# Queries of the third layer taken without waiting for scores, and the last attention item interleaved with the out blocks by halves

## The chip, the cores and the metric

One core of one Trainium2 chip runs one program. The metric is the device time of one execution in microseconds; the kernel before took 1414.33 us (median of 3 runs, 1413.99 to 1415.4). TensorE, ScalarE, VectorE and GpSimd are called PE, ACT, DVE and POOL below, as in the profile; SP is the queue that issues the weight loads.

## The reference, cut to what matters

Activations x have 4 images of 16 x 16 tokens with 1024 channels. Four layers follow each other, each `x = x + layer(group_norm(x))`.

```python
# layer 0: lambda layer     # layer 1: masked attention, 16 heads of 64, then Wo
# layer 2: attention, 16 heads of 64, with relative positions in rows and columns
qkv = x @ qkv_w + qkv_b
attn = (q * hd**-0.5) @ k.T            # per image and head, 256 x 256
rel_h = einsum('bhwc,hkc->bhwk', q, Rh); rel_w = einsum('bhwc,wkc->bhwk', q, Rw)
attn = softmax(attn + rel_h[..., None] + rel_w[..., None, :])
out = (attn @ v) @ proj_w + proj_b
# layer 3: 3 x 3 convolution of every channel, then four small cores that are
# one 1024 x 1024 channel matrix M, bias, relu
```

The change touches layer 2 (the third) and the seam between it and layer 3.

## The kernel before

Channels lie on partitions, tokens along the free dimension. Float32 products are made of three matmuls (high by high, low by high, high by low), so a weight block of 128 output channels by 1024 inputs costs 8 chunks of 3 matmuls over 512 tokens. Weights come in half blocks of 128 x 512 (4 chunks), through three slots of SBUF: SP loads the raw half block once POOL has split the one before it in that slot, POOL splits it into high and low (L212, L214) once PE has finished with the slot (`w_wait_used`), and PE waits for `w_ready`. The order of the half blocks is the list `sources`, written by `take`, and SP, POOL and PE all go through it in that order.

Attention of layers 1 and 2 is 32 items of two heads by two images: four stages of 8 items, stages 0 and 1 for layer 1 and stages 2 and 3 for layer 2. After a stage's 8 items come its 8 out blocks (`out_block(s, o, chunks)`), whose sums DVE adds to xT (`add_out`, L1403), with the statistics of the next group norm (`stats_of`) behind each.

Each engine's order is written out by hand. PE runs item i as: scores(i, 0), Q of item i+1 (`project`), transposes of the values (`turn_values`), the rest of Q, transposes of the probabilities (`turn_probs`, L1096), part of K, `attend(i, 0)` (L1112), scores(i, 1) (L1076), `relative(i + 1)` (64 small matmuls, L1140 and L1141), the rest of K, and V. `relative(i + 1)` waits for `q_hi`, which ACT raises when it has copied the queries of item i+1 from bank 0 to qp (`evac_q`, L1264). ACT runs item i as: evac_v, evac_o(i - 1), exps(i, 0), evac_t(i, 0) (the transposed probabilities), evac_q(i + 1), exps(i, 1) and so on; evac_q first waits for `s_done` of all scores of item i:

```python
            product_done(act, (i, "Q"))
            if i:
                act.wait_ge(s_done, 4 * i)
```

The last item (31) has no next item. There PE runs scores(31, 0), the rest of V, scores(31, 1), and then pieces of out blocks 0 and 1 of stage 3 between the transposes and products of the item. scores(31, 1) waits for `p_exp`, exps(31, 0) on ACT, which stand behind evac_v(31) and evac_o(30). Out blocks of stage 3 alternate between PSUM banks 0 and 1, so block o waits for the sum of block o - 2. Into blocks 2 to 7 the building of M is woven: `build_m(k)`, 16 pieces of two matmuls (L1168) into banks 4 and 5, two after the first half of a block and one after the second; ACT takes the high part (`head_of_m`, L1500), DVE the low part (`rest_of_m`, L1507), and piece k waits for the low part of piece k - 2. POOL makes the factors in BD (`masked_factor`, L1491), one for every four pieces.

Then PE runs `channel_product(0)` to `(3)` (L1534, 96 matmuls each) with `convolution` (L1551) between. Products of image 0 use banks 0 to 3 and wait for all sums of stage 3 on banks 0 and 1. DVE and ACT first do the group norm of images 2 and 3 (statistics, coefficients, then 8 times y, head, rest: L381, L379, L387, L392), and only then take image 0's products out of PSUM (L1586, L1612); channel_product(1) waits for that, bank by bank (`u_lo`).

Of the kernel before, what the change touches and what calls it, by code (L numbers as in the profile page):

```python
# [30 lines left out]
CK = C // P  # L31
HALF = 512
PAIRS = 8
# [32 lines left out]
def build(nc, A, out):  # L66
    outer = ExitStack()
    with outer:
# [98 lines left out]
        def take_item(i, halves=range(2)):  # L167
            for kind in "QKV":
                take((i, kind), STAGES[i // PAIRS][0], kind, i % PAIRS, halves)
# [3 lines left out]
        for i in range(ITEMS):  # L173
            if i + 1 < ITEMS:
                take_item(i + 1)
            if i % PAIRS == PAIRS - 1:
                for o in range(CK):
                    take((i // PAIRS, "O", o), STAGES[i // PAIRS][0], "O", o)

        slot_of, turn_of, landed_at, before_it = [], [], [], []  # L180
# [495 lines left out]
def later_layers(nc, A, out, outer, g):  # L676
# [301 lines left out]
    def layer_of(i):  # L978
        return STAGES[i // PAIRS][0]
# [26 lines left out]
        return PT if (i, kind) == (0, "V") else PJ[kind]  # L1006

    def out_bank(s, o):
        return (0 if s == 3 else O) + o % 2

    def product_done(eng, key):
        w_wait_used(eng, slots[key, 1])
# [1 line left out]
    def attention_pe(pe):  # L1014
# [128 lines left out]

        def out_block(s, o, chunks):
            for c in chunks:
                if c == 0 and o >= 2:
                    pe.wait_ge(sum_done, CK * s + o - 1)
                if c == 0 and o == 0 and s < 3 or o < 2 and c == CK - 1:
                    pe.wait_ge(o_hi, PAIRS * (s + 1))
                    pe.wait_ge(o_lo, PAIRS * (s + 1))  # L1150
                if c == 0 and o == 1 and s in (1, 2):
                    pe.wait_ge(relh_evac, PAIRS * (s - 1) + 1)
                    pe.wait_ge(relw_evac, PAIRS * (s - 1) + 1)
                if c == 0 and o == 0 and s == 3:
                    pe.wait_ge(v_evac, ITEMS)
                    pe.wait_ge(o_hi, ITEMS - 1)
                    pe.wait_ge(o_lo, ITEMS - 1)
                chunk_of((s, "O", o), c, lambda hl, c: (oh, ol)[hl][:, c, :], out_bank(s, o))

        def build_m(i):  # L1160
            if i >= 16:
                return
            if i % 4 == 0:
                pe.wait_ge(bd_ready, i // 4 + 1)
            if i >= 2:
                pe.wait_ge(m_lo, i - 1)
            for s in range(2):
                m = nc.tensor.matmul(PS[:, PT + i % 2, s * 256:s * 256 + 256], BD[:, (i // 4) % 2, (2 * i + s) % 8, :],  # L1168
                                     ttA[:, :], start=True, stop=True)
            m.then_inc(m_done, 1)  # L1170
# [31 lines left out]
        attend(i - 1, 1)  # L1202
        scores(i, 0)
        project(i, "V", range(4, CK))
        scores(i, 1)
        out_block(3, 0, range(0, 3))
        turn_values(i)
        turn_probs(i, 0)
        out_block(3, 0, range(3, 6))
        attend(i, 0)  # L1210
        out_block(3, 0, range(6, 7))
        out_block(3, 1, range(0, 2))
        turn_probs(i, 1)
        out_block(3, 1, range(2, 4))
        attend(i, 1)
        out_block(3, 1, range(4, 7))
        for o in range(2):
            out_block(3, o, range(7, CK))
        for o in range(2, CK):
            out_block(3, o, range(0, 4))  # L1220
            for k in range(2):
                build_m(3 * (o - 2) + k)
            out_block(3, o, range(4, CK))
            build_m(3 * (o - 2) + 2)

    def attention_act(act):
        def evac_v(i):
# [19 lines left out]
        def evac_t(i, a):  # L1247
            w = P * len(tiles(i))
            for n in (4 * i + 2 * a, 4 * i + 2 * a + 1):
                act.wait_ge(t_done, n + 1)  # L1250
                if n >= 4:
                    act.wait_ge(o_done, n // 2 - 1)
                nc.scalar.activation(probT[:, n % 4, 0:w], PS[:, PT + n % 2, 0:w], ACT.Copy).then_inc(t_evac, 1)  # L1253

        def evac_q(i):
            if i == ITEMS:
                return
            product_done(act, (i, "Q"))
            if i:
                act.wait_ge(s_done, 4 * i)  # L1260
            if layer_of(i) == 1:
                nc.scalar.activation(qh, PS[:, PJ["Q"], :], ACT.Copy).then_inc(q_hi, 1)
            else:
                nc.scalar.activation(qp, PS[:, PJ["Q"], :], ACT.Identity, bias=bias[:, i % PAIRS:i % PAIRS + 1]).then_inc(q_hi, 1)  # L1264
# [37 lines left out]
        for i in range(ITEMS):  # L1302
            evac_v(i)
            if i % PAIRS:
                evac_o(i - 1)
            exps(i, 0)
            evac_t(i, 0)
            evac_q(i + 1)
            exps(i, 1)
            evac_relative(i + 1)  # L1310
            evac_k(i + 1)
            evac_t(i, 1)
            if i % PAIRS == PAIRS - 1:
                evac_o(i)
            if 1 <= i % PAIRS <= 4:
                for c in (2 * (i % PAIRS) - 2, 2 * (i % PAIRS) - 1):
                    norm.y(nc.scalar, i // PAIRS + 1, c)
                for c in (2 * (i % PAIRS) - 2, 2 * (i % PAIRS) - 1):
                    norm.head(i // PAIRS + 1, c)
# [11 lines left out]
    def attention_dve(dve):  # L1331
# [81 lines left out]
        for i in range(ITEMS):  # L1413
            s, j = i // PAIRS, i % PAIRS
            maxima(i, 0)
            if j:
                rest_of_o(i - 1)
            normalize(i, 0)
            take_v(i)
            if j == 0:  # L1420
                norm.group_stats(s + 1)
            maxima(i, 1)
            rest_of_q(i + 1)
            normalize(i, 1)
            take_relative(i + 1)
            if i + 1 < ITEMS:
                rest_of_k(i + 1)
            if j == PAIRS - 1:
                rest_of_o(i)
            if j == 0:  # L1430
                norm.coefficients(s + 1)
            if 1 <= j <= 4:
                for c in (2 * j - 2, 2 * j - 1):
                    norm.y(nc.vector, s + 1, c)
                for c in (2 * j - 2, 2 * j - 1):
                    norm.rest(s + 1, c)
            if j == PAIRS - 1:
                for o in range(CK):
                    if s == 3 and o >= 2:
                        rest_of_m(dve, 3 * (o - 2))  # L1440
                        rest_of_m(dve, 3 * (o - 2) + 1)
                    add_out(s, o)
                    if o:
                        stats_of(s, o - 1)
                    if s == 3 and o >= 2:
                        rest_of_m(dve, 3 * (o - 2) + 2)
                stats_of(s, CK - 1)
                norm.aggregate(s + 2, range(CK), 16)

# [12 lines left out]
    def attention_pool(pool):  # L1462
        for n in range(SLOTS0 + 2, len(sources)):
            w_split(pool, n)
            if n == slots[(1, "Q"), 0]:
                pool.wait_ge(w_ready, n + 1)
                nc.gpsimd.memset(qa[64:96, :, :], 0.0).then_inc(zeroed, 1)
                pool.wait_ge(zeroed, 1)
            for s in range(4):
                if n == slots[(PAIRS * s + 1, "K"), 0]:  # L1470
                    norm.power(s + 1)
            if n == slots[(ITEMS - 4, "Q"), 0]:
                masked_factor(pool, 0)
                masked_factor(pool, 1)
            for k in (2, 3):
                if n == slots[(3, "O", 0), 0] + 4 * k:
                    masked_factor(pool, k)
        norm.power(5)


# [19 lines left out]
        nc.scalar.activation(hi, src, ACT.Copy).then_inc(m_hi, 1)  # L1500

    def rest_of_m(dve, i):
        if i >= 16:
            return
        dve.wait_ge(m_hi, i + 1)
        src, hi, lo = m_views(i)
        nc.vector.tensor_tensor(lo, src, hi.bitcast(F32), ALU.subtract).then_inc(m_lo, 1)  # L1507
# [11 lines left out]
    def last_pe(pe):  # L1519
        pe.wait_ge(m_lo, 16)  # L1520

        def channel_product(b):
            for tt in range(2):
                for half in range(2):
                    bank = 2 * tt + half
                    if b:
                        pe.wait_ge(u_lo, 4 * (b - 1) + bank + 1)
                    elif bank < 2:
                        pe.wait_ge(sum_done, 4 * CK)
                    for c in range(CK):  # L1530
                        if b == 2 and bank == 0:
                            norm.ready(5, c)
                        for k, (hl, w) in enumerate(((0, Mh), (0, Ml), (1, Mh))):
                            m = nc.tensor.matmul(PS[:, bank, :], x3(hl, b, c, tt * P), w[:, c, half * HALF:half * HALF + HALF],  # L1534
                                                 start=c == k == 0, stop=c == CK - 1 and k == 2)
                    m.then_inc(u_done, 1)
# [260 lines left out]
```

## Time and profile before

| | |
|---|---|
| median of 3 runs | 1414.33 us |
| profiled execution | 1415.18 us, of it span 1413.4 us |
| PE busy | 1346.5 us, 95% of the span |
| DVE, ACT, POOL busy | 44%, 31%, 44% |
| mean granted TensorE clock | 0.989 |
| 16 waits of L1140 on ACT L1264 | 13.4 us |
| from the end of V's matmuls of item 31 to the end of the last out block | 61.0 us |

Matmul ends in the trace are modelled: a matmul of 512 columns shows about 0.40 us, while the next starts 0.23 us after it. So distances below are taken from start to start; for a group of n matmuls with one duration, the last start is the group's end less one duration.

### The profile page before, as it was taken

How to read it: one execution, taken by the hardware profiler on the slowest of the kernel's cores; microseconds unless marked ns; L12 is line 12 of the kernel's file. 1: busy time of each engine (PE TensorE's matmuls, PEld its weight loads, DVE VectorE, ACT ScalarE, POOL GpSimd, SP SyncE). 2: the span in 40 equal slices, each digit the busy share in tenths (PEclk: the TensorE clock that was granted, in tenths of full speed). 3: DMA queues.
4: the chain of work that ended last, by engine and by line, in shares of the span. 5: the costliest groups of instructions: out<-in, count | busy, mean ns of one | idle time of the engine just before them, and what ended most of it. 6: DMA issues, size and time to landing. Idle time of an engine off the chain costs nothing.

```text
span 1413.4 us, 20625 instructions
## 1 busy us (share of the span) xinstructions
PE 1346.5 (95%) x7792; PEld 1055.7 (75%) x7792; DVE 617.2 (44%) x1385; ACT 439.1 (31%) x1053; POOL 626.4 (44%) x715
## 2 busy tenths in 40 slices
PE   4899889799999999999999999999999999999998
PEld 3688755468888888888888777777877777677787
DVE  6423422674655324565423354433244444347322
ACT  2220112033534302353320344434024444334222
POOL 2332179035555466455556444434654534445100
PEclk9999989999999999999999999999999999999999
DMA  5111135012222232222223211211321212111012
GB/s 191 38 46 45 30 64 88 0 46 77 75 61 76 69 95 83 68 71 65 75 74 91 61 53 60 60 54 55 91 72 62 59 53 61 53 53 31 1 52 68
DMA packets 57122, 89.23 MB, mean 63 GB/s; under 512 B 6880, under 2 KB 19840, under 8 KB 57024
## 3 DMA queue, kind: packets, MB, share of 16 engines
q1 hardware_dynamic: 55024, 84.59, 21.3%
q10 hardware_dynamic: 2000, 3.32, 0.7%
q8 instruction: 63, 1.03, 0.3%
q14 instruction: 35, 0.29, 0.1%
HBM read 79.50 MB, written 4.19 MB: 59 GB/s over the span
## 4 chain that ended last, share of the span: by engine, by line
PE 82%; DVE 2%; ACT 1%; issue 1%; POOL 0%; ACTq 0%; DVEq 0%; POOLq 0%
PE PS L1022 50%; PE PS L1534 5%; PE PS L1076 4%; PE PS L1096 3%; PE PS L858 3%; PE PS L1112 2%; PE PS L876 2%; PE PS L1064 2%; PE PS L864 2%; PE PS L1122 2%; PE PS L1141 2%; PE PS L1551 2%; DVE part L842 1%; PE PS L1087 1%; ACT part L1264 1%
## 5 line engine op out<-in xcount | busy, mean ns | idle before, releaser
L1022 PE MATMUL PS<-XB,w_hi 128*128 128x512 f32 x1024 | 354.0, 405 | 1.0 <-POOL w_lo L214 1.0
L212 POOL CAST w_hi<-w_raw 128x512 fp32r<-128x512 f32 x195 | 123.0, 631 | 407.7 <-PE PS L1022 296.9
L214 POOL TENSOR_TENSOR w_lo<-w_raw,w_hi 128x512 fp32r<-128x512 f32 x195 | 254.3, 1304 | 15.6
L1022 PEld LDWEIGHTS PS<-XB,w_hi 128*128 128x128 f32 x1024 | 192.5, 188 | 44.4 <-issue 2.1
L1022 PE MATMUL PS<-XB,w_lo 128*128 128x512 f32 x512 | 202.2, 395 | 0.0
L1022 PE MATMUL PS<-XB,part 128*128 128x512 f32 x768 | 199.3, 403 | 0.0
L1022 PEld LDWEIGHTS PS<-XB,part 128*128 128x128 f32 x768 | 140.8, 188 | 30.5
L1243 ACT ACTIVATE part<-PS,nmax 128x256 f32<-128x256 f32 (+1 forms) x256 | 111.0, 448 | 165.6 <-DVE nmax L1340 108.7
L212 POOL CAST part<-part 128x512 fp32r<-128x512 f32 x85 | 53.0, 623 | 155.8 <-PE PS L1022 155.8
L1340 DVE TENSOR_REDUCE nmax<-PS 128x2 f32<-128x512 f32 x64 | 43.9, 690 | 170.0 <-PE PS L1076 170.0
L1022 PE MATMUL PS<-part,w_hi 128*128 128x512 f32 x344 | 112.8, 396 | 1.6 <-POOL w_lo L214 1.6
L214 POOL TENSOR_TENSOR part<-part,part 128x512 fp32r<-128x512 f32 x85 | 111.0, 1306 | 6.8
L1253 ACT ACTIVATE part<-PS 128x384 f32<-128x384 f32 (+1 forms) x128 | 62.7, 543 | 163.6 <-PE PS L1096 163.6
L1022 PEld LDWEIGHTS PS<-XB,w_lo 128*128 128x128 f32 x512 | 96.5, 189 | 18.6 <-issue 0.2
L1337 DVE TENSOR_REDUCE nmax<-PS 128x1 f32<-128x128 f32 (+1 forms) x128 | 36.8, 350 | 153.1 <-PE PS L1069 153.1
L1350 DVE TENSOR_SCALAR part<-part,prec 128x256 f32<-128x256 f32 (+1 forms) x256 | 94.5, 411 | 4.5
L1022 PEld LDWEIGHTS PS<-part,w_hi 128*128 128x128 f32 x344 | 65.3, 190 | 16.2 <-DVE xT L1403 2.0
L635 PE MATMUL PS<-XB,w_hi 128*128 128x512 f32 x256 | 72.0, 398 | 0.0
L1022 PE MATMUL PS<-part,w_lo 128*128 128x512 f32 x172 | 67.5, 392 | 0.0
L1076 PE MATMUL PS<-part,part 112*128 112x256 f32 x256 | 63.8, 392 | 3.1 <-ACT part L1243 3.1
L392 DVE TENSOR_TENSOR XB<-part,XB 128x512 fp32r<-128x512 f32 x40 | 42.4, 1091 | 50.7 <-ACT XB L387 50.7
L1022 PE MATMUL PS<-part,part 128*128 128x512 f32 x252 | 61.0, 390 | 0.0
(142 smaller groups left out, 2010.8 us busy)
## 6 DMA issues: line engine op xcount, KB each, us to landing
w_raw<-in_w SPq DMA_DIRECT2D x187, 256.0 KB, 2.6
part<-in_w SPq DMA_DIRECT2D x85, 256.0 KB, 2.6
part<-part SPq DMA_DIRECT2D x32, 128.0 KB, 4.3
out_x<-xT SPq DMA_DIRECT2D x16, 256.0 KB, 2.1
xT<-in_x ACTq DMA_DIRECT2D x8, 256.0 KB, 7.9
xT<-in_x SPq DMA_DIRECT2D x8, 256.0 KB, 10.7
w_raw<-in_w SPq DMA_DIRECT2D x16, 128.0 KB, 4.0
part<-in_emb ACTq DMA_DIRECT2D x1, 961.0 KB, 12.4
```

Of the source, the lines that this page charges most:

```text
L212: pool.tensor_copy(hi, raw).then_inc(w_hi_done, 1)
L214: pool.tensor_tensor(lo, raw, hi.bitcast(F32), ALU.subtract).then_inc(w_ready, 1)
L635: m = nc.tensor.matmul(PS[:, 2 * (n % 2) + h, :], wt[:, (c % 4) * P:(c % 4) * P + P], x_part(hl, h, c), start=c == k == 0, stop=c == CK - ...
L858: m = nc.tensor.matmul(bank[:, 0:DY * SIDE], lhs, rhs, start=jp == 0, stop=jp == 1)
L1022: m = nc.tensor.matmul(PS[:, bank, :], wt[:, (c % 4) * P:(c % 4) * P + P], rhs(hl, c), start=c == k == 0, stop=c == CK - 1 and k == 2)
L1076: m = nc.tensor.matmul(PS[:, S + hh, qt * N:qt * N + N], qa[:, hh, qs], ka[:, hh, a * N:a * N + N], start=True, stop=True)
L1096: m = nc.tensor.transpose(PS[:, PT + n % 2, at:at + P], prob[:, n % 4, qt, kt_ * P:kt_ * P + P], ident[:, :])
L1243: last = nc.scalar.activation(prob[:, n % 4, qt, lo:hi], PS[:, S + n % 2, qt * N + lo:qt * N + hi], ACT.Exp, bias=nmax[:, n % 4, qt:qt + 1 ...
L1253: nc.scalar.activation(probT[:, n % 4, 0:w], PS[:, PT + n % 2, 0:w], ACT.Copy).then_inc(t_evac, 1)
L1340: last = nc.vector.tensor_reduce(nmax[:, n % 4, :], PS[:, S + n % 2, :].rearrange("p (a n) -> p a n", a=2), AX, ALU.max, negate=True)
L1350: last = nc.vector.tensor_scalar(prob[:, n % 4, qt, lo:hi], prob[:, n % 4, qt, lo:hi], prec[:, n % 4, qt:qt + 1], None, ALU.mult)
L1534: m = nc.tensor.matmul(PS[:, bank, :], x3(hl, b, c, tt * P), w[:, c, half * HALF:half * HALF + HALF], start=c == k == 0, stop=c == CK - 1 ...
```

## The change

In layer 2 ACT copies the queries without a wait for scores, and before evac_t(i, 0) instead of behind it. (The first item of layer 2, item 16, is taken during item 15.) For the last stage, the half blocks of out blocks 0 to 2 come as three first halves and then three second halves; the first three chunks of out block 0 stand ahead of scores(31, 1); out blocks use three banks, 1, 7 and 0, in turn (block o waits for the sum of block o - 3, block 1 for the copy of the values out of bank 7); the 16 pieces of M follow the table M_AFTER; two of POOL's factors move in its queue; and image 0's products wait for the sums bank by bank.

```diff
@@ -173,8 +173,12 @@
         for i in range(ITEMS):
             if i + 1 < ITEMS:
                 take_item(i + 1)
+            if i == ITEMS - 1:
+                for half in range(2):
+                    for o in range(3):
+                        take((3, "O", o), 2, "O", o, (half,))
             if i % PAIRS == PAIRS - 1:
-                for o in range(CK):
+                for o in range(3 if i == ITEMS - 1 else 0, CK):
                     take((i // PAIRS, "O", o), STAGES[i // PAIRS][0], "O", o)
 
         slot_of, turn_of, landed_at, before_it = [], [], [], []
@@ -1006,7 +1010,11 @@
         return PT if (i, kind) == (0, "V") else PJ[kind]
 
     def out_bank(s, o):
-        return (0 if s == 3 else O) + o % 2
+        return (1, X, 0)[o % 3] if s == 3 else O + o % 2
+
+
+    M_AFTER = {(0, 0): (), (1, 0): (), (2, 0): (), (0, 1): (0, 1), (1, 1): (2, 3), (2, 1): (4, 5), (3, 0): (6,), (3, 1): (7,),
+               (4, 0): (8,), (4, 1): (9,), (5, 0): (10, 11), (5, 1): (12,), (6, 0): (13,), (6, 1): (14,), (7, 0): (15,), (7, 1): ()}
 
     def product_done(eng, key):
         w_wait_used(eng, slots[key, 1])
@@ -1143,23 +1151,23 @@
 
         def out_block(s, o, chunks):
             for c in chunks:
-                if c == 0 and o >= 2:
-                    pe.wait_ge(sum_done, CK * s + o - 1)
-                if c == 0 and o == 0 and s < 3 or o < 2 and c == CK - 1:
+                beside = 3 if s == 3 else 2
+                if c == 0 and o >= beside:
+                    pe.wait_ge(sum_done, CK * s + o - beside + 1)
+                if c == 0 and o == 0 and s < 3:
                     pe.wait_ge(o_hi, PAIRS * (s + 1))
                     pe.wait_ge(o_lo, PAIRS * (s + 1))
+                if s == 3 and o == 0:
+                    pe.wait_ge(o_hi, PAIRS * s + c + 1)
+                    pe.wait_ge(o_lo, PAIRS * s + c + 1)
                 if c == 0 and o == 1 and s in (1, 2):
                     pe.wait_ge(relh_evac, PAIRS * (s - 1) + 1)
                     pe.wait_ge(relw_evac, PAIRS * (s - 1) + 1)
-                if c == 0 and o == 0 and s == 3:
-                    pe.wait_ge(v_evac, ITEMS)
-                    pe.wait_ge(o_hi, ITEMS - 1)
-                    pe.wait_ge(o_lo, ITEMS - 1)
+                if c == 0 and o == 1 and s == 3:
+                    pe.wait_ge(v_ready, ITEMS)
                 chunk_of((s, "O", o), c, lambda hl, c: (oh, ol)[hl][:, c, :], out_bank(s, o))
 
         def build_m(i):
-            if i >= 16:
-                return
             if i % 4 == 0:
                 pe.wait_ge(bd_ready, i // 4 + 1)
             if i >= 2:
@@ -1202,26 +1210,22 @@
         attend(i - 1, 1)
         scores(i, 0)
         project(i, "V", range(4, CK))
+        out_block(3, 0, range(0, 3))
         scores(i, 1)
-        out_block(3, 0, range(0, 3))
+        out_block(3, 0, range(3, 4))
         turn_values(i)
         turn_probs(i, 0)
-        out_block(3, 0, range(3, 6))
+        out_block(3, 1, range(0, 4))
         attend(i, 0)
-        out_block(3, 0, range(6, 7))
-        out_block(3, 1, range(0, 2))
+        out_block(3, 2, range(0, 2))
         turn_probs(i, 1)
-        out_block(3, 1, range(2, 4))
+        out_block(3, 2, range(2, 4))
         attend(i, 1)
-        out_block(3, 1, range(4, 7))
-        for o in range(2):
-            out_block(3, o, range(7, CK))
-        for o in range(2, CK):
-            out_block(3, o, range(0, 4))
-            for k in range(2):
-                build_m(3 * (o - 2) + k)
-            out_block(3, o, range(4, CK))
-            build_m(3 * (o - 2) + 2)
+        for o in range(CK):
+            for half in range(0 if o >= 3 else 1, 2):
+                out_block(3, o, range(4 * half, 4 * half + 4))
+                for k in M_AFTER[o, half]:
+                    build_m(k)
 
     def attention_act(act):
         def evac_v(i):
@@ -1256,9 +1260,9 @@
             if i == ITEMS:
                 return
             product_done(act, (i, "Q"))
-            if i:
-                act.wait_ge(s_done, 4 * i)
             if layer_of(i) == 1:
+                if i:
+                    act.wait_ge(s_done, 4 * i)
                 nc.scalar.activation(qh, PS[:, PJ["Q"], :], ACT.Copy).then_inc(q_hi, 1)
             else:
                 nc.scalar.activation(qp, PS[:, PJ["Q"], :], ACT.Identity, bias=bias[:, i % PAIRS:i % PAIRS + 1]).then_inc(q_hi, 1)
@@ -1304,8 +1308,11 @@
             if i % PAIRS:
                 evac_o(i - 1)
             exps(i, 0)
+            if i + 1 >= LO_KEYS:
+                evac_q(i + 1)
             evac_t(i, 0)
-            evac_q(i + 1)
+            if i + 1 < LO_KEYS:
+                evac_q(i + 1)
             exps(i, 1)
             evac_relative(i + 1)
             evac_k(i + 1)
@@ -1436,14 +1443,13 @@
                     norm.rest(s + 1, c)
             if j == PAIRS - 1:
                 for o in range(CK):
-                    if s == 3 and o >= 2:
-                        rest_of_m(dve, 3 * (o - 2))
-                        rest_of_m(dve, 3 * (o - 2) + 1)
+                    for k in M_AFTER[o, 0] if s == 3 else ():
+                        rest_of_m(dve, k)
                     add_out(s, o)
                     if o:
                         stats_of(s, o - 1)
-                    if s == 3 and o >= 2:
-                        rest_of_m(dve, 3 * (o - 2) + 2)
+                    for k in M_AFTER[o, 1] if s == 3 else ():
+                        rest_of_m(dve, k)
                 stats_of(s, CK - 1)
                 norm.aggregate(s + 2, range(CK), 16)
 
@@ -1472,9 +1478,10 @@
             if n == slots[(ITEMS - 4, "Q"), 0]:
                 masked_factor(pool, 0)
                 masked_factor(pool, 1)
-            for k in (2, 3):
-                if n == slots[(3, "O", 0), 0] + 4 * k:
-                    masked_factor(pool, k)
+            if n == slots[(3, "O", 3), 1]:
+                masked_factor(pool, 2)
+            if n == slots[(3, "O", 5), 0]:
+                masked_factor(pool, 3)
         norm.power(5)
 
 
@@ -1500,8 +1507,6 @@
         nc.scalar.activation(hi, src, ACT.Copy).then_inc(m_hi, 1)
 
     def rest_of_m(dve, i):
-        if i >= 16:
-            return
         dve.wait_ge(m_hi, i + 1)
         src, hi, lo = m_views(i)
         nc.vector.tensor_tensor(lo, src, hi.bitcast(F32), ALU.subtract).then_inc(m_lo, 1)
@@ -1525,8 +1530,8 @@
                     bank = 2 * tt + half
                     if b:
                         pe.wait_ge(u_lo, 4 * (b - 1) + bank + 1)
-                    elif bank < 2:
-                        pe.wait_ge(sum_done, 4 * CK)
+                    elif bank < 3:
+                        pe.wait_ge(sum_done, 4 * CK - 2 + bank)
                     for c in range(CK):
                         if b == 2 and bank == 0:
                             norm.ready(5, c)
```

## Rows read from the trace of the kernel before

**Rows 1.** Waits of PE over the whole span (total us, times, longest).
```profile
PE PS L1140 <- ACT part L1264: 13.4, 16, 0.8
```
**Rows 2.** Timeline of item 21: start, duration, instruction, [idle before it <- releaser].
```profile
917.33 0.40 PE L1022 MATMUL PS<-XB,w_hi 128*128 128x512 f32 x1
...
917.86 0.61 POOL L212 CAST w_hi<-w_raw 128x512 fp32r<-128x512 f32 x1 [1.25 <-PE PS L1022]
918.20 1.09 ACT L1253 ACTIVATE part<-PS 128x512 f32<-128x512 f32 x2 [4.66 <-PE PS L1096]
...
920.62 1.08 PE L1112 MATMUL PS<-part,part 128*64 128x256 f32 x8
...
923.72 0.69 ACT L1264 ACTIVATE part<-PS,bias 128x512 f32<-128x512 f32 x1 [4.44 <-PE PS L1076]
...
924.46 0.23 PE L1140 MATMUL PS<-part,part 128*48 128x32 f32 x1 [0.84 <-ACT part L1264]
```
**Rows 3.** PE's timeline just before that wait: the last two matmuls of scores.
```profile
923.03 0.59 PE L1076 MATMUL PS<-part,part 112*128 112x256 f32 x2
```
**Rows 4.** PE's timeline in stage 3: a change of tile shape without a wait.
```profile
1172.52 2.97 PE L1022 MATMUL PS<-XB,part 128*128 128x512 f32 x12
...
1175.41 1.08 PE L1112 MATMUL PS<-part,part 128*64 128x256 f32 x8
```
**Rows 5.** Timeline of PE and of ACT (one row) in item 31.
```profile
1231.07 3.16 PE L1022 MATMUL PS<-XB,part 128*128 128x512 f32 x12
...
1237.04 0.23 ACT L1243 ACTIVATION_READ_ACCUMULATOR part<-PS,nmax 128x1 f32 x1
...
1237.32 2.23 PE L1076 MATMUL PS<-part,part 112*128 112x256 f32 x8 [3.09 <-ACT part L1243]
1238.99 0.99 PE L1022 MATMUL PS<-part,w_hi 128*128 128x512 f32 x1
...
1242.81 0.60 PE L1087 MATMUL PS<-ident,part 128*128 128x128 f32 x4
```
**Rows 6.** Two windows: us; busy PE, PEld, DVE, ACT, POOL; granted clock; DMA.
```profile
1239.50:1243.00 3.50, 3.50 (x12) 2.69 (x11) 0.00 (x0) 0.00 (x0) 0.00 (x0) 0.59 0.00 0
...
1258.10:1264.60 6.50, 6.46 (x31) 5.46 (x32) 2.00 (x2) 2.19 (x2) 5.51 (x7) 1.00 0.45 122
```
**Rows 7.** Timeline of POOL and PE at the seam of out blocks 1 and 2.
```profile
1256.20 0.39 PE L1022 MATMUL PS<-part,w_hi 128*128 128x512 f32 x1
...
1256.73 1.26 POOL L214 TENSOR_TENSOR w_lo<-w_raw,w_hi 128x512 fp32r<-128x512 f32 x1
...
1258.14 0.47 PE L1022 MATMUL PS<-part,w_hi 128*128 128x512 f32 x1 [1.56 <-POOL w_lo L214]
```
**Rows 8.** Timeline of DVE and ACT: values, first pieces of M, a sum.
```profile
1243.45 0.69 DVE L1358 COPY part<-PS 128x512 f32<-128x512 f32 x1 [5.33 <-PE PS L1087]
...
1261.42 2.19 ACT L1500 ACTIVATE part<-PS 128x512 fp32r<-128x512 f32 x2 [7.83 <-PE PS L1168]
...
1262.60 2.22 DVE L1507 TENSOR_TENSOR part<-PS,part 128x512 fp32r<-128x512 f32 x2 [4.57 <-ACT part L1500]
...
1264.72 0.75 DVE L1403 SCALAR_TENSOR_TENSOR xT<-PS,bias,xT 128x512 f32<-128x512 f32 x1
```
**Rows 9.** The chain that ended last: two pieces of M and one half block.
```profile
1261.14 0.47 PE PS L1168 x4
1261.62 2.77 PE PS L1022 x12
```
**Rows 10.** Timeline of PE and DVE from the last out block into layer 3.
```profile
1294.88 0.39 PE L1022 MATMUL PS<-part,w_hi 128*128 128x512 f32 x1
1296.20 22.62 PE L1534 MATMUL PS<-part,XB 128*128 128x512 f32 x96 [0.94 <-DVE xT L1403]
...
1318.76 1.88 DVE L1612 TENSOR_TENSOR XB<-PS,XB 128x512 fp32r<-128x512 f32 x3
...
1319.50 22.45 PE L1534 MATMUL PS<-part,XB 128*128 128x512 f32 x96 [0.67 <-DVE XB L1612]
```

## The prediction

> **What bounds the kernel now.** I read the busy shares first: PE is busy 95% of the span, the others under half of it. So PE's order is the kernel's length, and only what lets PE wait, or run at the lower clock, can be won. Second, the waits of PE [rows 1]: 16 waits of `relative` on ACT's copy of the queries, 13.4 us together, 0.84 us each, one for each item of the third layer. The last item has one of 3.09 us [rows 5]. Third, the timelines around these places, with the granted clock of the windows. They show two further losses near the end: after the 3.1 us the granted clock is 0.59 over 3.5 us [rows 6], a mix of the two levels (2.4 and 1.2 GHz), and out block 2 begins 1.94 us after the last matmul ahead of it, its weights being split too late [rows 7]. Last, the seam to layer 3 [rows 10]: PE waits 0.94 us for a sum, and 22 us later 0.67 us for DVE. The reader is to see there that the second wait is not made by PE's own work: DVE comes to L1612 only when the group norm of images 2 and 3 is through, and that begins with the last out block's sum.
>
> **Part one, the queries.** In item 21 the scores' last matmul starts at 923.03 + 0.59 - 0.39 = 923.23 (0.39 is the duration of one) [rows 3]. ACT copies the queries only then, 923.72 to 924.41, and `relative` starts at 924.46 [rows 2], 1.23 us after that last start. Q itself was finished long before: its last matmul started at 917.33, and POOL, which waits for the same event, ran at 917.86 [rows 2]. With the wait gone ACT copies at about 917.9 to 918.6. What stays is the step from one matmul to another of a different tile shape. The nearest row: from 128x128 to 128x64 the last start is 1172.52 + 2.97 - 0.40 = 1175.09 and the next 1175.41, so 0.32 us [rows 4]. The gain is 1.23 - 0.32 = 0.91 us an item, times 16 = **14.6 us**. Bounds: no less than the idle time itself, 0.84 x 16 = 13.4; no more than with the plain pitch of 0.23 us between starts, 1.0 x 16 = 16.0. I take the middle because `relative` uses columns 48 wide and so also changes the tile.
>
> The Trainium skill says that changing the tiling mode drains TensorE (TensorEngine Tiling (Array Packing), Key Properties). By that rule the first small matmul would wait for the modelled end of the scores, the gain would be the 0.84 us, and the total time 1.1 us more than mine; the row with 0.32 us shows a start 0.08 us before the modelled end, so it agrees only nearly.
>
> What is put in the way: the copy (0.69 us) now stands ahead of evac_t(i, 0), which ran 918.20 to 919.29 and would end at about 919.7. `attend(i, 0)` starts at 920.62 [rows 2], so 0.9 us of cover is left, and the copy costs nothing. Behind evac_q on ACT stand evac_t, exps(i, 1) and the copies of relative positions and keys; the exps start up to 0.7 us earlier than before, as ACT is free when the first maximum comes. PE's next need of them, turn_probs(i, 1), comes 7 us after relative starts and did not wait at all before. DVE's part of the queries still waits for the scores; V needs it only 15 matmuls (3.5 us) after `relative`. V, K, the weights and the norm's work hang on PE's progress and move with it. SP issues the same loads in the same order through here.
>
> **Part two, the last item and the out blocks.** The copy of V, evac_o(30) and the exps of item 31 end at 1237.27 before and after, so scores(31, 1) starts at 1237.32 again [rows 5]; V's last matmul started at 1231.07 + 3.16 - 0.40 = 1233.83. The three chunks of out block 0 (9 matmuls, 2.1 us) now run inside that hole, so the stall falls from 3.09 to about 0.95 us. Before, they ran behind it from 1238.99 to 1242.81 [rows 5], 3.82 us where 2.1 do at full clock, because the clock had been halved [rows 6]. All 3.82 us are saved there, if a stall of 0.95 us does not lower the clock; the stall of 1.56 us [rows 7] did not: the window behind it grants 1.00 [rows 6].
>
> The late weights: the two halves of block 0 and those of block 1 filled three slots for long, and block 2 had to wait for block 0's second half, then for POOL's 0.6 + 1.3 us [rows 7]. With the halves in the order 0a 1a 2a 0b 1b 2b, each slot comes free at least one PE piece of 2.8 us before its next half is wanted: 0b's split starts when 0a is through (about 1240), 1b's after 1a (1244), 2b's after 2a (1248.7), and they are wanted at 1249.8, 1253 and 1256.5. That saves 1.94 - 0.23 = 1.71 us. SP's loads for them are issued one split earlier and have landed by then.
>
> New waits. Block 1 waits for the copy of the values (bank 7): the copy starts 0.64 us after turn_values and takes 0.69 [rows 8], turn_values and the transposes behind it take 1.2 us, so 0.15 us. Pieces of M: from a pair's start (1261.14 [rows 9]) ACT is through with both at 1263.61 and DVE at 1264.82 [rows 8], 3.68 us later. The first pairs follow each other after 0.47 + 2.77 us [rows 9], their second piece after 3.5, so it waits some 0.2 us; in the next pair DVE also has a sum and statistics of 0.7 us each in front [rows 8], which makes it about 0.3. From out block 3 on there is mostly one piece per half block, and DVE's 1.85 us of work fit in PE's 3.0. I take 0.5 us for M; the ends are 0 and 3.2 (both of DVE's 0.75 us wholly in the way, 1.6 us for each of two pairs). The amount of matmuls is the same. Waits on three banks are met: the sum of block o - 3 is over two blocks old. POOL's factors for pieces 8 and 12 come over 8 us before PE wants them.
>
> Sum of part two: 3.82 + 1.71 - 0.15 - 0.5 = **4.9 us**.
>
> **The seam to layer 3: nothing.** Image 0's products start 1.1 us earlier after the last block (1294.88 + 0.23 for 1296.20 [rows 10]). But channel_product(1) waits for DVE at 1319.50, and DVE's chain, from the last block's sum through norm, coefficients and eight rounds of y, head and rest, keeps its 24.6 us from the last matmul of block 7. So the wait at 1318 grows from 0.67 to about 1.76 us and takes the gain back.
>
> **The sum.** 14.6 + 4.9 = 19.5 us off. The profiled execution took 1415.18, 1.8 us of it outside the span, and it lies 0.85 us above the median. From the median: 1414.33 - 19.5 = **1394.8 us**.
>
> **Rivals.**
> 1. The clock falls in the last item all the same, or in the longer wait at the seam. For it: 3.09 us of stall did it. Against: 1.56 us did not [rows 6, 7]. Price: 3.82 us less the 2.1 of full clock, 1.7 us once, 3.4 twice: 1396.5 to 1398.2.
> 2. Relative's wait is only partly won: something else, such as the copy or evac_t, is late by some tenths in many items. Each 0.1 us is 1.6 us; with half of the gain lost 1402. Against: 0.9 us of cover [rows 2].
> 3. The other side: evac_q blocks ACT's queue in front of evac_t(i, 0). If Q's last matmul were seen by ACT later than by POOL, attend(i, 0) would stand still; past the 0.9 us of cover each microsecond costs 16, and at 2.1 us late it eats the 19.5; at 2.5 us late the time is 1420. The POOL row at 917.86 speaks against it.
> 4. The seam gives its 1.1 us after all, if DVE's chain is shorter than I read: 1393.7.
> 5. M's pieces wait for DVE by the upper end: 1397.5.
>
> **Chances.** Forecast 0.72 (its own range 1392.5 to 1396.2), rival 1 0.09, rival 2 0.07, rival 3 0.02, rival 4 0.04, rival 5 0.06. The range 1392 to 1398.5 leaves out rival 3 and most of rival 2. What a measurement can tell here from no change is 0.2%, 2.8 us: only rival 3 and an extreme of rival 2 come near it. Faster 0.95, same 0.02, slower 0.03.
>
> **What would show it.** Right: no waits of L1140 on ACT; the copy (L1264's successor) 0.5 us after Q's last matmul; from scores' last start to relative's first 0.32 us; one wait of about 0.95 us for the exps of item 31 and clock 1.00 behind it; no wait on POOL; waits for DVE at M of some tenths; none on the sum at the seam and 1.7 us on DVE before channel_product(1). Wrong: attend waiting for L1253, a granted clock under 1 after 1230 us, or out blocks whose distance from V's last start to block 7's last is not 61.05 - 4.9 = 56.1 us.

## The result, and the profile after

The changed kernel takes 1396.62 us (median of 4 runs, 1395.68 to 1397.51), the kernel before 1414.29 (4 runs): a ratio of 0.9874, 95% interval 0.9856 to 0.9891. That is 17.7 us less, with 15.4 to 20.4 inside the interval. Forecast were 1394.8 us and 19.5 us less. The median lies inside the whole range (1392 to 1398.5), but 0.4 us outside the forecast's own (1392.5 to 1396.2), next to the price of rival 1 (1396.5). The profiled execution took 1396.11 us with a span of 1394.3, so by the traces the change is worth 19.1 us. On another chip, where both ran again (e12 below), the medians lie 19.5 us apart, 1396.04 us being the changed kernel's.

The waits of PE after its first 680 us:

```profile
PE PS L1539 <- DVE XB L1617: 1.8, 1, 1.8
PE PS L1084 <- ACT part L1247: 1.0, 1, 1.0
PE PS L1176 <- DVE part L1512: 0.2, 1, 0.2
```

The 16 waits on ACT's copy of the queries [rows 1] are gone. Item 21's timeline shows what took their place:

```profile
912.17 0.40 PE L1030 MATMUL PS<-XB,w_hi 128*128 128x512 f32 x1
...
912.61 0.69 ACT L1268 ACTIVATE part<-PS,bias 128x512 f32<-128x512 f32 x1 [4.23 <-PE PS L1030]
...
913.19 1.08 ACT L1257 ACTIVATE part<-PS 128x512 f32<-128x512 f32 x2
...
915.46 1.08 PE L1120 MATMUL PS<-part,part 128*64 128x256 f32 x8
916.48 1.99 PE L1084 MATMUL PS<-part,part 112*128 112x256 f32 x8
...
918.40 0.23 PE L1148 MATMUL PS<-part,part 128*48 128x32 f32 x1
```

ACT copies 0.44 us after Q's last matmul starts. The scores' last matmul starts at 916.48 + 1.99 - 0.39 = 918.08, relative's first at 918.40: 0.32 us, where it was 1.23 [rows 2, 3]. Fourteen further items show this step within 0.01 us; in the first (item 16), behind other matmuls, it is 0.15 where it was 1.06. The copy of the transposed probabilities ends at 914.27, well ahead of `attend` at 915.46.

Item 31 (PE, and one row of ACT), the answer to [rows 5]:

```profile
1216.72 3.15 PE L1030 MATMUL PS<-XB,part 128*128 128x512 f32 x12
...
1222.67 0.23 ACT L1247 ACTIVATION_READ_ACCUMULATOR part<-PS,nmax 128x1 f32 x1
...
1222.96 1.99 PE L1084 MATMUL PS<-part,part 112*128 112x256 f32 x8 [1.04 <-ACT part L1247]
1224.61 0.59 PE L1030 MATMUL PS<-part,w_hi 128*128 128x512 f32 x1
1225.03 0.40 PE L1030 MATMUL PS<-part,w_lo 128*128 128x512 f32 x1
...
1225.50 0.60 PE L1095 MATMUL PS<-ident,part 128*128 128x128 f32 x4
1225.93 1.04 PE L1104 MATMUL PS<-ident,part 128*128 128x128 f32 x8
1226.88 0.50 PE L1030 MATMUL PS<-part,w_hi 128*128 128x512 f32 x1
...
1223.00:1226.00 3.00, 3.00 (x16) 2.61 (x17) 0.72 (x3) 0.00 (x0) 0.20 (x1) 1.00 0.26 85
```

V's last start to scores(31, 1) is 3.49 us as before, but 1.04 us of it is idle where 3.09 were. The scores take 1.99 us where they took 2.23, the granted clock behind the stall is 1.00 (last row, a window as in [rows 6]: third figure from the end), and turn_values comes 2.54 us after the scores' start, not 5.49.

Pieces 2 to 5 of M on PE, and the seam (PE, one row of DVE), the answer to [rows 10]:

```profile
1241.84 0.40 PE L1176 MATMUL PS<-ttA,part 96*128 96x256 f32 x2
1242.45 0.50 PE L1176 MATMUL PS<-ttA,part 96*128 96x256 f32 x2 [0.22 <-DVE part L1512]
1242.79 2.93 PE L1030 MATMUL PS<-part,part 128*128 128x512 f32 x12
1245.56 0.86 PE L1176 MATMUL PS<-ttA,part 96*128 96x256 f32 x4
1246.26 0.39 PE L1030 MATMUL PS<-part,w_hi 128*128 128x512 f32 x1
...
1275.89 0.40 PE L1030 MATMUL PS<-part,w_hi 128*128 128x512 f32 x1
1276.12 22.34 PE L1539 MATMUL PS<-part,XB 128*128 128x512 f32 x96
...
1299.49 0.68 DVE L1617 TENSOR_TENSOR XB<-PS,XB 128x512 fp32r<-128x512 f32 x1
1300.23 22.65 PE L1539 MATMUL PS<-part,XB 128*128 128x512 f32 x96 [1.76 <-DVE XB L1617]
```

The products of image 0 follow the last block at once (0.23 us), and PE stands still for 1.76 us in front of those of image 1, as forecast.

So that runs can be compared without what varies ahead of the change, each trace is cut at four starts on PE. S1 runs from the transposes of item 15 to V's second half of item 31; S2 from there to block 7's last matmul; S3 from there to channel_product(1); S4 from there to the span's end. What lies ahead of S1 should be one length in all kernels, and differs by up to 2.7 us among them (706.39 to 709.05), about as much as whole times of one kernel differ (1414.59 to 1417.54 in seven runs of the kernel before). All are differences of start times in us, but for the span's end, which is read to 0.1 us:

| kernel | ahead | S1 | S2 | S3 | S4 |
|---|---|---|---|---|---|
| before | 708.16 | 522.91 | 63.81 | 24.62 | 93.90 |
| changed | 708.50 | 508.22 | 59.17 | 24.34 | 94.07 |
| e1 | 707.41 | 508.22 | 65.07 | 24.33 | 94.07 |
| e2 | 708.32 | 522.92 | 59.16 | 24.63 | 93.97 |
| e3 | 706.98 | 508.21 | 59.17 | 24.34 | 95.50 |
| e4 | 708.06 | 513.61 | 59.17 | 24.35 | 94.11 |
| e4b | 708.45 | 508.22 | 59.16 | 24.62 | 95.65 |
| e5 | 709.05 | 508.22 | 59.16 | 24.35 | 94.12 |
| e7 | 707.90 | 508.22 | 62.92 | 24.34 | 95.52 |
| e8 | 708.36 | 508.22 | 58.46 | 24.34 | 94.12 |
| e12 (changed again) | 706.39 | 508.22 | 59.15 | 24.38 | 94.16 |
| e6, S3 and S4 together | 707.81 | 508.21 | 59.17 | 116.21 | |
| e9, the same | 708.59 | 508.22 | 58.54 | 116.35 | |
| e11, the same | 706.65 | 508.21 | 57.80 | 116.24 | |

The change: S1 14.69 us less, S2 4.64 less, S3 0.28 less, S4 0.17 more, and 0.34 more ahead of it all: 19.1 us.

### The profile page after: what moved, and what is told of

It reads as the page before. It is cut to its first block, busy times and chain, and to the rows that moved or that the text cites. A ratio compares the mean times of both kernels' runs of the same rounds, so it can differ in the third digit from the quotient of the medians.

```text
span 1394.3 us, 20607 instructions
## 1 busy us (share of the span) xinstructions
PE 1343.4 (96%) x7792; PEld 1054.4 (76%) x7792; DVE 643.6 (46%) x1385; ACT 438.8 (31%) x1053; POOL 626.5 (45%) x715
## 4 chain that ended last, share of the span: by engine, by line
PE 82%; DVE 2%; issue 1%; ACT 1%; POOL 0%; ACTq 0%; DVEq 0%; POOLq 0%
PE PS L1030 50%; PE PS L1539 5%; PE PS L1084 4%; PE PS L1104 4%; PE PS L862 3%; PE PS L1120 2%; PE PS L880 2%; PE PS L1072 2%; PE PS L868 2%; PE PS L1130 2%; PE PS L1149 2%; PE PS L1556 2%; DVE part L846 1%; PE PS L1095 1%; PE PS L1077 1%
## 5 line engine op out<-in xcount | busy, mean ns | idle before, releaser
L1030 PE MATMUL PS<-XB,w_hi 128*128 128x512 f32 x1024 | 353.9, 405 | 1.0 <-POOL w_lo L218 1.0
L1357 DVE TENSOR_SCALAR part<-part,prec 128x256 f32<-128x256 f32 (+1 forms) x256 | 116.0, 495 | 4.5
L639 PE MATMUL PS<-XB,w_hi 128*128 128x512 f32 x256 | 72.1, 398 | 0.0
L622 PE MATMUL PS<-XB,w_hi 128*128 128x512 f32 x128 | 35.6, 428 | 24.9 <-ACT XB L297 19.6
```

The source lines that it names most:

```text
L639: m = nc.tensor.matmul(PS[:, 2 * (n % 2) + h, :], wt[:, (c % 4) * P:(c % 4) * P + P], x_part(hl, h, c), start=c == k == 0, stop=c == CK - ...
L1030: m = nc.tensor.matmul(PS[:, bank, :], wt[:, (c % 4) * P:(c % 4) * P + P], rhs(hl, c), start=c == k == 0, stop=c == CK - 1 and k == 2)
L1357: last = nc.vector.tensor_scalar(prob[:, n % 4, qt, lo:hi], prob[:, n % 4, qt, lo:hi], prec[:, n % 4, qt:qt + 1], None, ALU.mult)
```

## The experiments

**e1, the queries alone.** The kernel before, with only this:

```diff
             product_done(act, (i, "Q"))
-            if i:
-                act.wait_ge(s_done, 4 * i)
             if layer_of(i) == 1:
+                if i:
+                    act.wait_ge(s_done, 4 * i)
...
             exps(i, 0)
+            if i + 1 >= LO_KEYS:
+                evac_q(i + 1)
             evac_t(i, 0)
-            evac_q(i + 1)
+            if i + 1 < LO_KEYS:
+                evac_q(i + 1)
```

> The kernel before with the change of the queries alone (no wait for scores, copy ahead of evac_t), the last item and the out blocks as before. My theory: the two parts add, and this one is worth the distance that the trace of the changed kernel shows, 14.7 us: 1399.6 us where the kernel before takes 1414.3, with 0.32 us from the scores' last start to relative's first in all 16 items, and the 3.09 us wait, the halved clock and the 1.94 us at out block 2 still there. Rival (something else is late in part of the items): less than 13.4 us. Rival (the parts overlap): less than 14 here and the same for the rest.

Measured: 1400.98 us, ratio 0.9898 (0.9883 to 0.9913) to 1415.64 of the kernel before on that chip: 14.7 us less. S1 is the changed kernel's to the hundredth. S2 is not that of before but 1.26 us longer, so it is partly chance that the whole times differ by just what S1 gives. Windows of e1 at the end of its stall of 3.09 us and behind it (granted clock third from the end), and the scores there:

```profile
1218.00:1222.00 4.00, 0.91 (x5) 0.42 (x3) 1.62 (x5) 3.00 (x10) 1.88 (x2) 0.88 0.06 5
1222.00:1226.00 4.00, 4.00 (x10) 3.15 (x11) 0.64 (x3) 0.00 (x0) 0.00 (x0) 0.50 0.22 60
...
1221.87 3.78 PE L1076 MATMUL PS<-part,part 112*128 112x256 f32 x8 [3.09 <-ACT part L1243]
```

In the trace of before the clock fell after the scores had begun, and they took 2.23 us [rows 5]; here it fell ahead of them and they took 3.78. The same stall costs one or the other.

**e2, the rest alone.** The changed kernel with e1's edit taken back.

> The changed kernel with the queries' copy put back as it was: wait for the scores, behind evac_t. My theory: 56.4 us from V's last start to block 7's last start as in the changed kernel (61.05 before), the 16 waits of 0.84 us back, the time 4.6 to 5 us under before: about 1409.5. If the last item owed some of its gain to the earlier queries, less than 4.

Measured: 1410.1 us, ratio 0.9961 (0.9946 to 0.9976) to 1415.64: 5.5 us less. S1 is that of before (522.92), S2 that of the changed kernel (59.16). The two parts add, stretch by stretch; the 1.26 us of clock in e1's S2 belong to neither.

**e3, no wait, same place.** The changed kernel, with evac_q behind evac_t(i, 0) as before:

```diff
             exps(i, 0)
-            if i + 1 >= LO_KEYS:
-                evac_q(i + 1)
             evac_t(i, 0)
-            if i + 1 < LO_KEYS:
-                evac_q(i + 1)
+            evac_q(i + 1)
```

> The changed kernel with the copy of the queries left behind evac_t(i, 0), without the wait. My theory: only the wait mattered; the copy then runs 1.1 us later, still 4 us before relative, so no difference to the changed kernel (within 0.3 us in the span). The rival, that the place ahead of evac_t is needed: the waits of relative come back in part, up to 13 us.

Measured: 1396.26 us, ratio 0.9863 (0.9846 to 0.9879). S1 508.21: the place ahead of evac_t is worth nothing, the wait was all. In its item 21 the copy runs behind evac_t and still over 3 us before the scores are through:

```profile
911.52 1.09 ACT L1257 ACTIVATE part<-PS 128x512 f32<-128x512 f32 x2 [4.66 <-PE PS L1104]
912.49 0.69 ACT L1268 ACTIVATE part<-PS,bias 128x512 f32<-128x512 f32 x1
```

Its S4 is 1.43 us longer than the changed kernel's; that is taken up under the clock below.

**e4 and e4b, how much cover.** The changed kernel with three copies more (one in e4b), into a tile that nobody reads:

```diff
             else:
+                for k in range(3):
+                    nc.scalar.activation(spare[:, k, :], PS[:, PJ["Q"], :], ACT.Copy)
                 nc.scalar.activation(qp, PS[:, PJ["Q"], :], ACT.Identity, ...)
```

> The changed kernel with three further ACT copies of the queries' bank (into a spare tile that nobody reads) in each item of layer 2 ahead of the real one. Each takes 0.58 us in a row, so evac_t(i, 0) is 1.74 us later. The trace of the changed kernel shows 1.14 us of cover between evac_t's end and attend(i, 0). My theory: attend waits 0.6 us in each of 16 items, 9.6 us slower than the changed kernel, about 1406. If ACT's queue has more cover than I read (attend waits for something else anyway): no difference. If the rest of ACT's chain (exps) is late too: more than 15.

> The changed kernel with one further ACT copy of 0.49 us ahead of the queries' in each item of layer 2. With three, attend(i, 0) came 0.33 us later, which leaves 1.13 us of cover. My theory: one copy lies wholly in the cover, the distance from the transposes of item 15 to V of item 31 is the changed kernel's 508.2 us. If the cost were by copy and not by threshold: 1.8 us more.

Measured: e4 1401.3 us (ratio 0.9897, 0.9882 to 0.9912), S1 5.39 us longer than the changed kernel's; e4b one profiled run of 1397.98 us with S1 unchanged at 508.22. An item of e4 (ACT, PE):

```profile
916.19 1.10 ACT L1258 ACTIVATE part<-PS 128x512 f32<-128x512 f32 x2
...
916.70 0.40 PE L1031 MATMUL PS<-XB,w_hi 128*128 128x512 f32 x1
...
917.35 1.08 PE L1121 MATMUL PS<-part,part 128*64 128x256 f32 x8 [0.25 <-ACT part L1258]
```

K's last start to attend's first is 0.65 us, 0.33 more than without (915.46 - 915.14 in the changed kernel). evac_t ends 0.59 us after K's last start, there 0.87 us before it: three copies made it 1.46 us late, 0.49 each. So 1.46 - 0.33 = 1.13 us was cover: the threshold was where I read it (1.14), and I had the price of a copy wrong (0.58). It is a threshold and not a cost by copy, since one copy costs nothing.

**e5, the old wait for the sums.**

```diff
-                    elif bank < 3:
-                        pe.wait_ge(sum_done, 4 * CK - 2 + bank)
+                    elif bank < 3:
+                        pe.wait_ge(sum_done, 4 * CK)
```

> The changed kernel, but image 0's products wait for all sums of stage 3 again before their first bank. My theory: the chain through DVE sets the start of channel_product(1), so the wait of 0.9 to 1.1 us moves ahead of channel_product(0) and the one behind it falls from 1.76 to about 0.7; the distance from block 7's last start to channel_product(1)'s first stays at 24.3 us. The rival, that the bank by bank wait is worth its 1.1 us: 25.4.

Measured: one profiled run, 1396.67 us. PE's two products:

```profile
1277.75 22.62 PE L1539 MATMUL PS<-part,XB 128*128 128x512 f32 x96 [0.94 <-DVE xT L1410]
1300.78 22.66 PE L1539 MATMUL PS<-part,XB 128*128 128x512 f32 x96 [0.41 <-DVE XB L1617]
```

The wait only moves from one side of channel_product(0) to the other; S3 is 24.35 us, the changed kernel's 24.34. The second wait is 0.41 us and not the 0.7 expected, because channel_product(0), begun behind a wait, takes 22.62 us where it took 22.34.

**e6, POOL after the norm.** One line on POOL ahead of the convolution's matrix:

```diff
         product_done(pool, (3, "O", CK - 1))
+        pool.wait_ge(norm.lo, 6 * CK)
```

> The changed kernel, but POOL begins the convolution's matrix only after the last group norm is through (it waits for its eight low parts). In the changed kernel the first rounds of the norm, while POOL works, take 2.83 us each and the later ones 2.03, DVE's L396 1.49 us there and 0.69 later. My theory: DVE's chain gets about 3 us shorter, PE's wait of 1.76 us before channel_product(1) goes, and the time falls by about 1.7 us; POOL is through by about 1309, before the convolution asks at 1322. If POOL's work is not what slows the rounds: no difference.

Measured: 1393.52 us, ratio 0.9847 (0.983 to 0.9863) to 1416.42. DVE's second and third L396 of the norm in the changed kernel, then in e6:

```profile
1286.15 1.49 DVE L396 TENSOR_TENSOR part<-part,part 128x512 fp32r<-128x512 f32 x1 [0.28 <-ACT part L391]
...
1288.98 1.49 DVE L396 TENSOR_TENSOR part<-part,part 128x512 fp32r<-128x512 f32 x1 [0.27 <-ACT part L391]
```

```profile
1285.15 0.69 DVE L396 TENSOR_TENSOR part<-part,part 128x512 fp32r<-128x512 f32 x1 [0.79 <-ACT part L391]
...
1287.18 0.69 DVE L396 TENSOR_TENSOR part<-part,part 128x512 fp32r<-128x512 f32 x1 [0.79 <-ACT part L391]
...
1275.43 24.89 PE L1539 MATMUL PS<-part,XB 128*128 128x512 f32 x107
```

A round of the norm takes 2.03 us where it took 2.83 beside POOL's work. PE runs through from image 0 into image 1 (107 matmuls in a row in this window). S3 and S4 together are 2.20 us shorter, where 1.7 were expected; DVE's last L396 of the norm ends 2.3 us sooner after the last block, where 3 were expected. The Trainium skill says that GpSimd shares its SBUF interfaces with VectorE, with contention for VectorE instructions that read two SBUF inputs (GPSIMD Engine Reference, Specifications). L396 is one of these and the rows agree, 1.49 us against 0.69. It is not the only one: L385, the product with the norm's coefficients, takes 0.93 us beside POOL's work and 0.41 without it.

**e7, block 0 behind the scores again.**

```diff
-        out_block(3, 0, range(0, 3))
         scores(i, 1)
-        out_block(3, 0, range(3, 4))
+        out_block(3, 0, range(0, 4))
```

> The changed kernel, but the first three chunks of out block 0 stand behind scores(31, 1) again, all else left. My theory: the stall is 3.09 us again, the granted clock is halved behind it, and the distance from V's last start to block 7's last start grows by 2.1 us of uncovered stall and 1.6 of clock, from 56.4 to 60.1. If the halved clock came from something else (the order of the halves, the banks): 58.5.

Measured: one profiled run of 1400.7 us, S2 62.92, so 3.75 us longer; the granted clock is 0.59 behind the stall:

```profile
1222.00:1226.00 4.00, 3.64 (x9) 2.95 (x10) 1.03 (x4) 0.31 (x2) 0.00 (x0) 0.59 0.23 66
...
1222.36 3.46 PE L1084 MATMUL PS<-part,part 112*128 112x256 f32 x8 [3.08 <-ACT part L1246]
```

Of it 3.08 - 1.04 = 2.04 us are the stall that is uncovered again; the other 1.71 I put down to the clock.

**e8, a fourth chunk ahead of the scores.**

```diff
-        out_block(3, 0, range(0, 3))
+        out_block(3, 0, range(0, 4))
         scores(i, 1)
-        out_block(3, 0, range(3, 4))
```

> The changed kernel with four chunks of out block 0 ahead of scores(31, 1) in place of three. My theory: the stall of 1.04 us takes up the fourth chunk (0.7 us), so 0.7 us less: 55.7 us from V's last start to block 7's last. A rival: turn_values comes directly behind scores and nothing is won, because the transposes then wait for DVE's norm of the probabilities (0.2 us spare).

Measured: one profiled run of 1395.37 us; the stall is 0.36 us, S2 0.71 shorter.

**e9, e11 and e12: better than both.** e9 is e6 with e8. e11 is e9 with another table:

```diff
-    (1, 1): (2, 3), (2, 1): (4, 5), (3, 0): (6,), (3, 1): (7,),
-    (4, 0): (8,), (4, 1): (9,), (5, 0): (10, 11), (5, 1): (12,), (6, 0): (13,), (6, 1): (14,),
+    (1, 1): (2,), (2, 1): (3, 4), (3, 0): (5,), (3, 1): (6,),
+    (4, 0): (7,), (4, 1): (8,), (5, 0): (9, 10), (5, 1): (11,), (6, 0): (12, 13), (6, 1): (14,),
```

> The changed kernel with both mends: four chunks of out block 0 ahead of scores(31, 1), and POOL's matrix for the convolution begun only after the last group norm. My theory: the two gains lie in different stretches and add, 0.7 us in the last item and 1.8 us at the seam plus 0.4 behind it, so 2.9 us or more under the changed kernel on the same chip, and no stall at the seam that could lower the clock. If they overlap: no better than 2.2.

> The same two mends, and the pieces of M spread so that only one follows the second half of block 1 (2 pieces, 1, 2, then one for each half block, two at two later places). The trace of the changed kernel shows 0.48 and 0.23 us lost at its second and third pair. My theory: piece 2 no longer waits, so 0.5 to 0.7 us less than the other kernel from V's last start to block 7's last; if the pieces' copies pile up later instead: no difference.

> The changed kernel once more, on the same chip as the two with mends. The distances from V's last start to block 7's last (56.4 us) and from there to channel_product(1) (24.3 us) repeat within 0.05 us; whether the 1.76 us wait in front of it halves the clock is left to chance: two of seven traces with such a wait had it, at 1.4 us. Time 1395.5 to 1397.5.

Measured on one chip, the kernel before at 1415.53: the changed kernel again 1396.04 (1394.11 to 1396.18), ratio 0.9861 (0.9844 to 0.9877); e9 1393.35 (1392.11 to 1393.68), ratio 0.984 (0.9825 to 0.9855); e11 1391.77 (1390.75 to 1392.06), ratio 0.9829 (0.9814 to 0.9844). So e11 is 4.3 us faster than the changed kernel beside it, 23.8 faster than the kernel before. By the cut traces it wins 3.65 us over it from V of item 31 on (57.80 + 116.24 against 59.15 + 24.38 + 94.16). e9 wins 2.7 us by the medians and 2.8 by the traces, a little under the 2.9 expected: 0.6 in S2, where e8 won 0.7, and 2.2 behind it, as e6 did. e9 and e11 can't be told apart by their times alone, whose intervals overlap; the stretch S2 tells them apart. In e11 no piece of M waits. Its second block gets one piece, its third two:

```profile
1239.27 0.40 PE L1176 MATMUL PS<-ttA,part 96*128 96x256 f32 x2
1239.51 2.91 PE L1030 MATMUL PS<-part,part 128*128 128x512 f32 x12
1242.26 0.63 PE L1176 MATMUL PS<-ttA,part 96*128 96x256 f32 x4
1242.73 0.40 PE L1030 MATMUL PS<-part,w_hi 128*128 128x512 f32 x1
```

S2 is 57.80 us, 0.74 less than e9's 58.54 and 1.37 less than the changed kernel's.

## Why the prediction held, point by point

**The queries, 14.6 us.** S1 fell by 14.69, and e1 shows it alone. The step that carried it was the tile change of 0.32 us taken from [rows 4]; relative's row shows 0.32. By the drain rule of the Trainium skill (TensorEngine Tiling (Array Packing), Key Properties), as I had worked it, it would have been 13.4; relative starts at 918.40, 0.07 us before the modelled end of the scores (918.47), so the measurement is against waiting for the whole modelled end.

**The cover on ACT.** I gave 0.9 us, e4 shows 1.13. Nothing hung on it, because e3 shows that the copy didn't need the place ahead of evac_t at all. Rival 3 was a true threshold, out of reach.

**The last item, 3.82 us.** From the scores' start to turn_values fell by 5.49 - 2.54 = 2.95, with one chunk of 0.70 inside it: 3.65. The 0.17 missing is nearly all the first step behind the scores, 0.42 us where others are 0.23 (1224.61 to 1225.03): whichever chunk follows the scores has it, and I took it off with the rest of the 3.82. e7 shows this term undone, 3.75. The clock stayed at 1.00 behind the 1.04 us stall, in each of the eight traces that had one.

**The late weights, 1.71 us.** The wait on POOL at out block 2 [rows 7] is gone in all traces with the new order, and e2, without the queries' part, keeps it gone. No run changed this alone, so 1.71 us is the length of the wait in the trace of before and not a measured difference.

**Pieces of M, 0.5 us.** The two pairs cost 0.48 (1242.79 - 1241.84, less 0.47) and 0.23: 0.71. e11 wins 0.74 by spreading them. Values out of bank 7: 0.15 forecast, turn_probs to block 1 took 0.95 us where such a step takes 0.79: 0.16. These terms add up to 3.65 + 1.71 - 0.16 - 0.71 = 4.49, and S2 fell by 4.64, so 0.15 us has no term. In sum part two gave 4.6 us for 4.9; the distance that I had named as a sign, from V's last start to block 7's, is 56.4 us and not 56.1.

**The seam, nothing.** e5 shows it: the bank by bank wait is worth 0.01 us. The 0.28 us of S3 is no gain of the change: S3 comes in two lengths, 24.33 to 24.38 and 24.62 to 24.63; e4b, changed kernel in all of this stretch, has the longer one, and e1, kernel before in this stretch, the shorter. The lengths part in the fifth round of the norm, where ACT's part (L383) starts 17.09 us after block 7's last matmul in the changed kernel and 17.38 in e4b; why it does stays open. e6 shows the reason: PE there waits for DVE's norm, and only what shortens that shortens the kernel.

**Rival 1, the clock.** I held the stalls under 2 us to be harmless, from the one row of 1.56 us. The one in the last item was, but the longer wait at the seam is not always. In eight traces with 1.72 to 2.05 us of it, three show the clock at its lower level (1.2 GHz) for a time behind it, in the others it is 1.00. e3, where each window is a mean of the two levels, and then the changed kernel:

```profile
1298.70 24.06 PE L1536 MATMUL PS<-part,XB 128*128 128x512 f32 x96 [1.76 <-DVE XB L1614]
...
1298.70:1301.70 3.00, 3.00 (x10) 2.45 (x11) 1.74 (x3) 0.41 (x1) 0.00 (x0) 0.75 0.00 0
1301.70:1305.00 3.30, 3.30 (x12) 2.57 (x12) 0.00 (x0) 0.00 (x0) 0.00 (x0) 0.71 0.00 0
```

```profile
1301.00:1310.00 9.00, 9.00 (x40) 7.27 (x39) 0.96 (x2) 0.00 (x0) 0.00 (x0) 1.00 0.00 0
```

The 96 products of e3 take 24.06 us in place of 22.65; S4 is 95.50 to 95.65 us in the three (e3, e4b, e7) and 93.97 to 94.16 in the five. The rival was right with 1.4 to 1.5 us in three traces. The changed kernel's two traces have it not. Of its untraced runs there is only the mean granted clock, which is 0.988 in the traces of e3 and e4b and 0.990 or 0.991 in those of the changed kernel: one untraced run of e12 has 0.988 (1396.18 us), but two others have 0.990 and are as long (1396.13 and 1395.95). So the clock alone does not explain the distance of the medians to 1394.8; what does stays open, and the stretch ahead of the change, with its 2.7 us, is as large. The step of the forecast that failed is the argument that one harmless stall proves the next; its size is inside the range given.

## What to carry to other kernels

A wait that guards nothing on the path that it blocks (here a copy from PSUM behind scores that it has no part in) is worth its idle time plus what the pipeline regains: count from start to start, and take the step that remains from a like change of shape in the same trace. Before spending a gain, follow the next join: at the seam 1.1 us of PE's time vanished in DVE's norm, and a single wait for POOL, whose work had been slowing DVE, brought 2.2. The stalls that work can be moved into should be filled until they are gone, since a stall costs its length and sometimes the clock behind it.

## What was not expected of the hardware

Eight kernels or repeats with the same program from the seam on, and a stall of 1.7 to 2.05 us there, ran behind it at the full or, for a time, at the halved clock (three of eight), 1.4 to 1.5 us apart. They differ ahead of the seam, and no kernel was traced with both, so whether this is chance or something upstream was not shown. In all three traces with a stall of 3.1 us (before, e1, e7) the clock was halved at its end or behind it, but from different moments: the kernel before and e1, alike in S2, differ there by 1.26 us. And ACT's plain copies of 128x512 out of PSUM to a 16-bit tile came 0.49 us apart, where I had priced them at 0.58.
